# Three edits to a two-layer graph kernel: coarser signals, two gapped scratch tables, normalised rows made in SBUF

## The reference, cut to what matters

```python
xn  = layernorm(x)                                   # 6250 x 256
def gcn(h, W, b):                                    # self loops, symmetric normalisation
    deg = segment_sum(edge_weight, dst) + 1
    dis = rsqrt(deg)
    h = h @ W.T
    msg = h[src] * (dis[src] * edge_weight * dis[dst])[:, None]
    return segment_sum(msg, dst) + h * dis[:, None]**2 + b
def block(x, ...): return x + relu(gcn(layernorm(x) * g + bln, W, b))
gnn = block(block(xn, layer 6), layer 7) @ Wp.T + bp
# linear attention over all nodes, 8 heads: q, k, v, elu + 1, sum of k*v over nodes,
# then @ Wm, layernorm, concat with xn, @ W1, relu, @ W2, layernorm, + xn
y = x + gnn + mix(xn)
z = layernorm(y)
# 8 experts of 256 -> 512 -> 256 with gelu; each row takes the two with the highest gate score
out = y + sum over the 2 chosen experts of (gelu(z @ W1[e] + b1[e]) @ W2[e] + b2[e])
```

## Time and profile before

| | |
|---|---|
| median of 3 runs | 4627.75 us |
| the profiled execution's own time | 4629.68 us |
| its span, first to last instruction | 4627.9 us |
| busy: TensorE matmul / VectorE / ScalarE / GpSimd | 3726.9 / 2568.6 / 1222.4 / 3072.5 us |
| TensorE clock granted, mean over the span | 0.904 |
| bytes moved | 516.13 MB, of them 414.39 MB by GpSimd's gathers |

### The profile page before, as it was taken

The page is one execution under the profiler, slowest core; times in us unless marked ns, Lnnn a source line. Parts: engine busy times, 40 slices in busy tenths (PEclk is TensorE's granted clock), DMA queues, the critical chain, the costliest instruction groups (busy, mean ns, idle before and its releaser), DMA issues.

```text
span 4627.9 us, 97268 instructions
## 1 busy us (share of the span) xinstructions
PE 3726.9 (81%) x28168; PEld 3130.2 (68%) x28169; DVE 2568.6 (56%) x9071; ACT 1222.4 (26%) x3196; POOL 3072.5 (66%) x3182
## 2 busy tenths in 40 slices
PE   3885677777777777777766999999999998999998
PEld 2773555655556555656554787887888787888877
DVE  6664554554555554555543565665666565665655
ACT  0221001101011010111002444444444444444434
POOL 0003677777777777777775777777777777777772
PEclk8997788888888888888887999999999999999999
DMA  3003344444444444444443333333333333333331
GB/s 133 23 22 115 112 125 125 129 129 125 118 128 129 126 129 121 126 128 126 129 117 98 105 115 113 113 113 112 112 110 115 113 115 107 115 115 112 110 109 44
DMA packets 256504, 516.13 MB, mean 112 GB/s; under 512 B 61752, under 2 KB 154304, under 8 KB 256448
## 3 DMA queue, kind: packets, MB, share of 16 engines
q0 software_dynamic: 151680, 414.39, 31.0%
q1 hardware_dynamic: 104768, 101.19, 6.6%
HBM read 475.60 MB, written 39.71 MB: 111 GB/s over the span
## 4 chain that ended last, share of the span: by engine, by line
PE 43%; DVE 19%; issue 12%; POOL 12%; DMA 8%; DVEq 4%; ACT 3%; POOLq 0%; SPq 0%; ACTq 0%
PE bank L1084 41%; POOL gs L436 12%; DMA gr<-h_d,idx_r 7%; DVE ss L852 4%; DVEq L240 2%; DVE rstd L587 2%; PE bank L1106 2%; DVE rstd L586 1%; DVE rstd L588 1%; DVE st L595 1%; DVEq L852 1%; ACT L567 1%; DVE w L983 1%; ACT hT L567 1%; DVE u L604 1%
## 5 line engine op out<-in xcount | busy, mean ns | idle before, releaser
L436 POOL DMA_INDIRECT gs<-h_d,idx_all x3038 | 2952.1, 972 | 1324.2 <-issue 668.8
L1084 PE MATMUL bank<-gs,ss 128*128 128x256 f32 x6272 | 1604.3, 403 | 12.8 <-DMA gs<-h_d,idx_all 11.7
L1084 PEld LDWEIGHTS bank<-gs,ss 128*128 128x128 f32 x6272 | 1219.6, 202 | 193.8 <-DMA gs<-h_d,idx_all 22.5
L852 DVE TENSOR_SCALAR ss<-iw,dst_f,ew 128x128 f32<-128x128 f32 x3152 | 889.9, 357 | 117.9 <-PE bank L1084 64.4
L1084 PE MATMUL bank<-experts,w 128*128 128x256 f16 x4896 | 622.8, 281 | 24.5 <-DVE w L983 24.5
L1084 PE MATMUL bank<-w,experts 128*128 128x128 f16 x9792 | 614.0, 219 | 1.2 <-DVE w L989 1.2
L1084 PEld LDWEIGHTS bank<-w,experts 128*128 128x128 f16 x9792 | 570.4, 98 | 49.9 <-issue 16.6
L1084 PEld LDWEIGHTS bank<-experts,w 128*128 128x128 f16 x4896 | 478.6, 101 | 105.4 <-DVE w L983 33.8
L1084 PE MATMUL bank<-gr,sr 128*128 128x256 f32 x244 | 124.0, 603 | 497.8 <-DMA gr<-h_d,idx_r 497.6
L1084 PEld LDWEIGHTS bank<-gr,sr 128*128 128x128 f32 x244 | 51.6, 263 | 550.9 <-DMA gr<-h_d,idx_r 550.8
L567 ACT ACTIVATE hT<-bank,eb1c 128x128 f32<-128x128 f32 x816 | 233.4, 369 | 447.6 <-PE bank L1084 444.4
(11 more groups left out here) (249 smaller groups left out, 3954.4 us busy)
## 6 DMA issues: line engine op xcount, KB each, us to landing
gs<-h_d,idx_all POOLq DMA_INDIRECT x3038, 2.8
hself<-h_d SPq DMA_DIRECT2D x100, 128.0 KB, 2.2
ew_in<-in_eW SPq DMA_DIRECT2D x49, 168.0 KB, 2.3
out<-u SPq DMA_DIRECT2D x51, 128.0 KB
u<-xn_d SPq DMA_DIRECT2D x50, 128.0 KB, 3.3
h_d<-u SPq DMA_DIRECT2D x50, 128.0 KB
u<-x_d SPq DMA_DIRECT2D x50, 128.0 KB
u<-r_d SPq DMA_DIRECT2D x50, 128.0 KB
```

What stands on the lines that cost most here:

```text
L436: pool.indirect_dma_start(gs[:, n, :], None, table[:, :], bass.IndirectOffsetOnAxis(ap=idx_all[:, w, n:n + 1], axis=0)).then_inc(s[f"main_ ...
L852: m = dve.tensor_scalar(ss[:, slot + j, :], iw[:, :], dst_f[:, bass.ds(c, 1)], ew[:, bass.ds(c, 1)], ALU.is_equal, ALU.mult)
L1084: return pe.matmul(out_ap, lhsT, rhs, start=first, stop=last, **kw)
```

## The change

**Signals.** TensorE adds 1 to `main_used` after four products instead of after each, VectorE adds 1 to `main_set` for four matrices instead of 4, and the relu and gelu groups add 1 instead of 4. All waits are counted anew; a gather buffer counts as free when the whole group of four that its product lies in is done. **Tables.** `x1_d` and `r_d` get a gap of one row after every 32 rows, so a tile of 128 rows is an access of four blocks of 32 rows. **Normalised rows.** `xn_d` goes, with its 49 stores in stage 1 and 50 loads in stage 2. ScalarE makes the rows of the next window from the raw rows of `x` in stage 2 (`xn_window`), the raw tile is loaded one window earlier, and the sum of normalised and raw rows moves on VectorE from step k = 6 to step k = 1. **Layer norm.** The inverse root inside `layer_norm` has two dependent steps per Newton iteration instead of three, each with one instruction per tile. The inverse root elsewhere is as before.

```diff
+S_GROUPS = S_SLOTS // U
+SPREAD = 4
+SROWS = P // SPREAD
+SBLOCK = SPREAD * (SROWS + 1)
-LN_LINKS = 5 + 3 * NEWTON
+LN_LINKS = 5 + 2 * NEWTON
-        xn_d = nc.dram_tensor("xn_d", [(W + 1) * P, D], F32).ap()
-        x1_d = nc.dram_tensor("x1_d", [(W + 1) * P, D], F32).ap()
-        r_d = nc.dram_tensor("r_d", [(W + 1) * P, D], F32).ap()
+        x1_d = nc.dram_tensor("x1_d", [(W + 1) * SBLOCK, D], F32).ap()
+        r_d = nc.dram_tensor("r_d", [(W + 1) * SBLOCK, D], F32).ap()
+        def spread(table, start):
+            return table[bass.ds(start, SBLOCK), :].rearrange("(a b) d -> a b d", a=SPREAD)[:, 0:SROWS, :]
...
-            tile(0, 0)
-            with sp.Fori(0, (W - 1) // 2) as p:
-                tile(2 * p + 1, 1)
-                tile(2 * p + 2, 0)
...
-                sp.wait_ge(s["r_done"], w)
-                sp.dma_start(u2[:, :], x[bass.ds(here, P), :]).then_inc(s["x_again"], 16)
-                sp.wait_ge(s["xn1_tp"], w + 1)
-                sp.wait_ge(s["xn_kept"], w + 1)
-                sp.dma_start(u1[:, :], xn_d[bass.ds(after, P), :]).then_inc(s["xn_in"], 16)
+                sp.wait_ge(s["x_used"], w + 1)
+                sp.dma_start(u2[:, :], x[bass.ds(after, P), :]).then_inc(s["x_in_again"], 16)
...
-                sp.dma_start(x1_d[bass.ds(here, P), :], u5[:, :]).then_inc(s["x1_out"], 16)
+                sp.dma_start(spread(x1_d, store_x), u5[:, :]).then_inc(s["x1_out"], 16)
-                sp.dma_start(r_d[bass.ds(after, P), :], u6[:, :]).then_inc(s["r_out"], 16)
+                sp.dma_start(spread(r_d, store_r), u6[:, :]).then_inc(s["r_out"], 16)
...
-                sp.dma_start(u2[:, :], r_d[bass.ds(here, P), :]).then_inc(s["r_in"], 16)
+                sp.dma_start(u2[:, :], spread(r_d, load_r)).then_inc(s["r_in"], 16)
-                sp.dma_start(u1[:, :], x1_d[bass.ds(nxt, P), :]).then_inc(s["x1_in"], 16)
+                sp.dma_start(u1[:, :], spread(x1_d, load_x)).then_inc(s["x1_in"], 16)
...
-                            pool.wait_ge(s["main_used"], g * STATIC + 1 + S_SLOTS)
+                            pool.wait_ge(s["main_used"], g * PIECES + 1 + S_GROUPS)
                         elif g:
-                            pool.wait_ge(s["main_used"], (g - 1) * STATIC + n + 2 + S_SLOTS)
+                            pool.wait_ge(s["main_used"], (g - 1) * PIECES + (n + 1) // U + 1 + S_GROUPS)
...
+            def xn_window(w):
+                act.wait_ge(s["x_in_again"], 16 * (w + 1))
+                act.activation(u1[:, :], u2[:, :], ACT.Identity, scale=rstd_w[:, bass.ds(w, 1)],
+                               bias=shift_w[:, bass.ds(w, 1)]).then_inc(s["xn_made"], 1)
...
                 act.copy(nT[:, :, :], half(5)).then_inc(s["mnT_set"], 1)
+                xn_window(w + 1)
                 act.wait_ge(s["hh_ps"], w + 1)
                 act.wait_ge(s["y1_ps"], w)
                 for j in range(HBLK):
-                    act.activation(hT[0][:, j, :], bank[6][:, j * P:(j + 1) * P], ACT.Relu,
-                                   bias=w1bias[:, j:j + 1]).then_inc(s["hr_done"], 1)
+                    a = act.activation(hT[0][:, j, :], bank[6][:, j * P:(j + 1) * P], ACT.Relu, bias=w1bias[:, j:j + 1])
+                a.then_inc(s["hr_done"], 1)
...
-            inv_sqrt(dve, ch, var, minus_half, rs, tmp)
+            dve.tensor_scalar(minus_half, raw, EPS, -0.5, ALU.add, ALU.mult)
+            ch.link(dve.tensor_scalar(var, raw, EPS, None, ALU.add))
+            ch.link(dve.tensor_scalar(rs.bitcast(I32), var.bitcast(I32), 1, None, ALU.arith_shift_right))
+            ch.link(dve.tensor_scalar(rs.bitcast(I32), rs.bitcast(I32), -1.0, float(RSQRT_BITS), ALU.mult, ALU.add))
+            for _ in range(NEWTON):
+                for i in range(n):
+                    one = slice(i, i + 1)
+                    last = dve.tensor_scalar(tmp[:, one], rs[:, one], rs[:, one], minus_half[:, one], ALU.mult, ALU.mult)
+                ch.link(last)
+                for i in range(n):
+                    one = slice(i, i + 1)
+                    last = dve.scalar_tensor_tensor(out=rs[:, one], in0=tmp[:, one], scalar=1.5, in1=rs[:, one], op0=ALU.add,
+                                                    op1=ALU.mult)
+                ch.link(last)
...
-                    if k == 6:
-                        dve.wait_ge(s["x_again"], 16 * (w + 1))
+                    if k == 1:
+                        dve.wait_ge(s["x_in_again"], 16 * (w + 1))
                         dve.wait_ge(s["xn_kept"], w + 1)
                         tc.link(dve.tensor_tensor(t_c[0][:, :], xn_keep[:, :], u2[:, :], ALU.add))
+                        dve.sem_inc(s["x_used"], 1)
...
-                    mm(acc, ss[:, q % S_SLOTS, :], gs[:, q - 1 if q else OWN - 1, :], fresh and q == 0, True,
-                       skip_group_check=True).then_inc(s["main_used"], 1)
+                    m = mm(acc, ss[:, q % S_SLOTS, :], gs[:, q - 1 if q else OWN - 1, :], fresh and q == 0, True,
+                           skip_group_check=True)
+                m.then_inc(s["main_used"], 1)
...
-                        pe.wait_ge(s["xn_in"], 16 * (w + 2))
+                        pe.wait_ge(s["xn_made"], w + 2)
```

More of the change, by code:

```diff
@@ L289, in _ @@
             sp.wait_ge(s["consts"], N_CONSTS)
-            for table, b in ((xn_d, W), (h1_d, 0), (h1_d, W + 1), (h2_d, W + 1), (x1_d, W), (r_d, 0)):
+            for table, b in ((h1_d, 0), (h1_d, W + 1), (h2_d, W + 1)):
                 sp.dma_start(rows(table, b), zero_tile[:, :]).then_inc(s["blank_out"], 16)
[L294 to L297, removed]
-            tile(0, 0)
-            with sp.Fori(0, (W - 1) // 2) as p:
-                tile(2 * p + 1, 1)
-                tile(2 * p + 2, 0)
+            for table, b in ((x1_d, W), (r_d, 0)):
+                sp.dma_start(spread(table, b * SBLOCK), zero_tile[:, :]).then_inc(s["blank_out"], 16)
             sp.wait_ge(s["dis_set"], 1)
@@ L313, in _ @@
                              xh[:, g * XG:(g + 1) * XG, :]).then_inc(s["h1_out"], 16)
-            sp.wait_ge(s["blank_out"], 16 * 6)
+            sp.wait_ge(s["blank_out"], 16 * 5)
             sp.wait_ge(s["kv_acc"], W)
             sp.wait_ge(s["h1_out"], 16 * (W // XG))
-            for b in range(2):
-                sp.wait_ge(s[f"xn_out{b}"], 16 * ((W + 1 - b) // 2))
             sp.sem_inc(s["table1"], 1)
             sp.dma_start(hself[:, :], rows(h1_d, 1)).then_inc(s["self_in"], 16)
-            sp.dma_start(u1[:, :], rows(xn_d, 0)).then_inc(s["xn_in"], 16)
+            sp.dma_start(u2[:, :], x[0:P, :]).then_inc(s["x_in_again"], 16)
             with sp.Fori(0, W) as w:
                 here, after, after2 = sp.snap(w * P), sp.snap((w + 1) * P), sp.snap((w + 2) * P)
+                store_x, store_r = sp.snap(w * SBLOCK), sp.snap((w + 1) * SBLOCK)
                 piece = sp.snap(w * EW_STEP)
@@ L349, in _ @@
             sp.wait_ge(s["self_in"], 16 * (W + 1))
-            sp.wait_ge(s["xn_in"], 16 * (W + 1))
+            sp.wait_ge(s["x_in_again"], 16 * (W + 1))
+            sp.wait_ge(s["xn_made"], W + 1)
             sp.wait_ge(s["xn1_tp"], W + 1)
@@ L353, in _ @@
             sp.dma_start(hself[:, :], rows(h2_d, 1)).then_inc(s["self2_in"], 16)
-            sp.dma_start(u1[:, :], rows(x1_d, 0)).then_inc(s["x1_in"], 16)
+            sp.dma_start(u1[:, :], spread(x1_d, 0)).then_inc(s["x1_in"], 16)
             def out_tile(w):
@@ L361, in r_tile @@
                 sp.wait_ge(s["x3_done"], w)
-                sp.dma_start(u2[:, :], rows(r_d, w)).then_inc(s["r_in"], 16)
+                sp.dma_start(u2[:, :], spread(r_d, w * SBLOCK)).then_inc(s["r_in"], 16)
             with sp.Fori(0, W) as w:
-                here, nxt, nxt2 = sp.snap(w * P), sp.snap((w + 1) * P), sp.snap((w + 2) * P)
+                here, nxt2 = sp.snap(w * P), sp.snap((w + 2) * P)
+                load_x, load_r = sp.snap((w + 1) * SBLOCK), sp.snap(w * SBLOCK)
                 sp.wait_ge(s["x3_done"], w)
-                sp.dma_start(u2[:, :], r_d[bass.ds(here, P), :]).then_inc(s["r_in"], 16)
+                sp.dma_start(u2[:, :], spread(r_d, load_r)).then_inc(s["r_in"], 16)
                 sp.wait_ge(s["acc2_read"], w + 1)
@@ L739, in _ @@
             inv_sqrt(dve, ch, w_s1[:, :], w_s2[:, :], rstd_all[:, :], w_s3[:, :])
+            dve.memset(rstd_w[:, W:W + 1], 0.0)
+            dve.memset(shift_w[:, W:W + 1], 0.0)
             ch.link(dve.scalar_tensor_tensor(out=shift_all[:, :], in0=mean_all[:, :], scalar=-1.0, in1=rstd_all[:, :],
```

55 lines of the change are left out of this document (29 added, 26 removed).

## The result

The changed kernel takes 4658.0 us (median of 4 runs, 4655.55 to 4661.15), the kernel before 4628.2 us beside it (4 runs, 4624.11 to 4632.79). The ratio is 1.0065 with a 95% interval of 1.0047 to 1.0082: slower by some 30 us. The prediction was 4623 us with a range of 4592 to 4656, so its likeliest case (no change) was wrong, and its range ends 2 us short of the time. The change has four parts; the title counts three, and the one that it leaves out, the layer norm, turns out to matter.

A forecast was written before the change was run, and what follows sets the result against it. GpSimd's issuing of gathers was taken to bound both layers. The terms 4627.9 + 0 (stage 1) + 0 (layer 1) + 0.3 - 5 + 0.5 gave 4623.7 us of span; forecast 4623 us, range 4592 to 4656.

The forecast's parts named there:

- likeliest case: Whole kernel: GpSimd keeps the pace, time 4623 us, spanning 4605 to 4640; chance 0.60, of which 0.38 within 9 us.
- the rival that decides "from 2.46 us of lateness on TensorE": Layer 2, each window's start: late output store and r load make TensorE set the pace, +98 us, 4721 us; chance 0.15.
- the sign "no wait of TensorE for the rest gather in layer 2": Layer 2, window ends: this wait, 2.46 us before, vanishing would show the prediction wrong and TensorE setting the pace.
- Signals, 0: Both layers: GpSimd's wait for up to three products more, at most 1.4 us, stays hidden; TensorE gains 0.
- The rivals on signals: GpSimd waits for the coarser signal, +1.4 us each, or fewer increments shorten the 0.305 us gap, 10 us per hundredth.
- Layer norm, +0.6 us of margin: VectorE, one-tile norm: three iterations each lose a 0.195 us link, 0.6 us less; 0 directly; two-tile gain about nil.
- Normalised rows, 0: Stages 1 and 2: dropped stores and loads, added ScalarE work and the moved sum cost 0, except +0.3 us in layer 1's last window.
- both fit in 5.64 us: Layer 1: ScalarE's 0.6 us instruction and VectorE's 0.9 us earlier sum stay within TensorE's 5.64 us wait for the rest gather.
- Gapped tables, direct cost 0 plus 0.5 in the tail: x1 and r transfers: longer landings stay within layer 2's margin of 2.46 us, 0 directly; +0.5 us in the tail.
- the four-engine case: Gapped transfers: each block keeps to its own engine, four carry 32 rows each instead of 16 carrying 8; 1.9 us more.
- Indirect term, -5 us: Layer 2: splits moved by 1.15 us against the gathers change the stretch by 0.1 us per window, 49 windows, -5 us.
- the same lottery lost: Layer 2: moved splits stretch gathers 1.95 us per window, 96 us, +30, 4656 us; chance 0.07 together with signal waits.

The follow-up runs named there:

- 16 blocks: The changed kernel with the tables gapped every 8 rows instead of every 32: 4638.0 us, ratio 1.0022.
- the two memsets: The kernel before with one useless memset ahead of layer 2's norm, 256 columns wide in one run, 768 in the other: 4635.3 and 4617.2 us.
- the split in pieces: The float16 split in two or four instructions in the kernel before: 4613.9 and 4610.4 us; in two in the changed kernel: 4635.4 us.

## Why the prediction was wrong

**The bound: right, its margin misread.** GpSimd's issuing sets the pace in both layers, before and after. In the window shown TensorE came 1.40 us later where 1.15 was predicted. But TensorE's wait for the rest gather is not the margin that the prediction took it for. It differs by window (before: over 2 us in 27 of 49, none in 10), and with the tables alone it is gone in 48 of 49 windows while GpSimd keeps its pace. So the rival that decides "from 2.46 us of lateness on TensorE" and the sign "no wait of TensorE for the rest gather in layer 2" do not hold; how late TensorE may come is not measured.

**Signals, 0: right** (4629.1 against 4628.7). The rivals on signals fall with it: no wait of GpSimd grew, and the gap stayed 0.30 us.

**Layer norm, +0.6 us of margin: mis-sized.** The timeline of the changed kernel:

```profile
3035.22 0.27 DVE L615 TENSOR_SCALAR rstd<-rstd 128x1 f32<-128x1 f32 x1
3035.52 0.16 DVE L619 SCALAR_TENSOR_TENSOR rstd<-rstd 128x1 f32<-128x1 f32 x1
3035.72 0.27 DVE L615 TENSOR_SCALAR rstd<-rstd 128x1 f32<-128x1 f32 x1
```

The new first step takes 0.27 us, not 0.16, so an iteration is 0.50 us where three links were 0.585: 0.26 us saved, not 0.6. The two-tile norm of layer 1, put at about nil, is 0.47 us longer (3.07 us instead of 2.59 from the statistics to the first normalised tile). Directly it is worth nothing either way, as predicted.

**Normalised rows, 0, and layer 1's stretch, not in the sum: wrong.** The step was "both fit in 5.64 us". They do, for TensorE (its median wait for the rest gather of layer 1 is 4.31 us, before 5.63). But moving work on VectorE moves its instructions with two SBUF tiles onto gathers, and a gather held at its start is not covered by TensorE's margin, because GpSimd is the bound. I had read the rule of the earlier trace rows off a float16 split and applied it to float16 splits and layer 2 only. Layer 1's own two-input instructions follow it too: its stretch is 21.8 us with this part alone, 19.1 with the norm or the tables alone, 23.8 in the whole, against 13.9. Which instruction is hit depends on the combination: with the rows alone the split of the edge weights, with the norm alone the product, with both the product and the sum.

**Gapped tables, direct cost 0 plus 0.5 in the tail: mis-sized.** What stands behind them comes 1.8 to 2.0 us later (the load of ew_in, L1018's wait), as the four-engine case had it at 1.9. The place I did not price is the end of layer 2, where GpSimd stands idle for the rest gather: 3.5 us in the last one, 4.3 in all, and 1.2 in the tail.

That four engines carry such a tile was taken as a case. No trace names the engine of a packet, but the packets of hardware queue 1 fit it. Each of the 49 stores of x1 is 128 packets of 1 KB and 16 of 4 B in the kernel before and with 16 blocks, and 128 and 4 in the changed kernel; the whole trace of the changed kernel has 239848 packets and that with 16 blocks 242248, 12 more for each of 200 transfers. At most 5 to 7 packets of the store run at once instead of 15 to 21, and from the first start to the last end they take 1.95 us (median) where they took 0.79: 1.17 us more, where the case had 1.25 and, with the gathers beside it, 1.9. In 16 blocks it is 0.74. Behind four blocks the ew_in load lands after 4.1 us, behind 16 blocks after 2.8, behind contiguous stores after 2.3.

**Indirect term, -5 us: the step that failed.** Layer 2's stretch went up by 10.4 us. The mechanism was right, and the sign was drawn from a table of one window with a shift taken as 1.15 us for all windows. The experiments show how much hangs on less than that: the tables' shift alone took 27 us of stretch away, 0.26 us less norm on top of it gave 36 back, 0.27 us of memset changed nothing, 0.70 took 20. The rival "the same lottery lost" (4656 us, counted at 0.07 together with the signal waits) is the one that came true in kind. In size it is a third of it: 10.4 us in layer 2 instead of 30. That the time is near its 4656 us is luck, since the rest comes from layer 1 and the ends of the stages.

An honest forecast from those rows would have given the stretch both signs with equal weight, and layer 1's as well. Of the 27.6 us of span, 20.3 are stretch, 5.5 are waits at the end of layer 2 and the tail, and 3.4 are start-up and change of layers, which in the other runs vary as much without regard to the edit; layer 1's other parts give 0.6 and layer 2's 1.0 back. Against the predicted span of 4623.7 us the miss is 31.8: 15.4 from the indirect term (+10.4 instead of -5), 9.9 from layer 1's stretch, 4.3 from the waits of layer 2, 0.7 from the tail, 3.1 from start-up and change of layers, less the 1.6 given back.

That the phase decides is shown for layer 2 (the old norm put back, the two memsets, the split in pieces). For layer 1 it is shown that three of the four parts raise the stretch, each alone, which instructions hold it, and that putting the old norm back changes which these are; no run moved one of them by itself.

## What to carry to other kernels

When one engine's issue rate is the bound, margins of the other engines say nothing about work that holds that engine's own instructions, and a neighbour's wait is not its margin until a run has used it up: list every instruction of the neighbour that can hold it, in all stages, before calling a move free. Where the hold depends on which instructions coincide, an edit of a quarter of a microsecond per window can be worth 30 us, as here, and single-part runs can't be added; judge such edits by the stretch and treat their time as a draw. The way out of the draw is to make the hold shorter (pieces of the long instruction), which gained 15 to 19 us in the kernel before and 23 in the changed one.

## What the runs showed of the hardware

In these traces a gather that starts early inside a VectorE instruction with two SBUF tiles is held until a fixed point of it and then takes its usual 0.95 us. In the kernel before and the changed one that point lies 0.54 to 0.58 us after the start of a 512-column split that the profile shows as 0.69, 0.38 for 336 columns, 0.28 to 0.30 for 256. Of two back-to-back pieces of 256 columns it waits for the first or for both (held to 0.28 and to 0.62 us in the two hits shown). In the kernel before, 75 gathers start in the first 0.15 us of a split and are lengthened by 0.41 us on average; 44 start so in L977, with one tile in SBUF and one in PSUM, and are not lengthened. L852, with one SBUF tile, holds some too, but briefly: of 687 gathers that start in it (it has two per-row operands besides), 159 are lengthened by more than 0.03 us, by 0.08 on average, and L852 has most of layer 1's stretch in the kernel before (8.2 of 13.9 us). Single gathers are lengthened by up to 0.57 us in the kernel before (1.513 against 0.946) and 0.69 in the changed one, where the gather started 0.13 us ahead of the split. The runs show which instructions hold a gather and how long, not by what.

A gapped tile cost SyncE more to issue: 0.57 us for L368 in four blocks, 0.56 in 16, 0.33 contiguous. So the issue time went with the gap, and the landing of the load behind with the number of blocks (4.1 us behind four, 2.8 behind 16, 2.3 contiguous).

In the changed kernel the VectorE operation on one column with two per-row operands takes 0.27 us (L615, 591 times), those with constants 0.14 to 0.15 (L608 to L611).

One chip ran the same program 1.42 times slower (6559 against 4628 us), with TensorE idle for no visible reason and a granted clock of 0.82 instead of 0.90. Its cause is left open.
